# A graph network kernel: gathers without a clear in front, for the first window groups of two layers

## What is computed

```python
edge_index = jnp.stack([src, dst])
x = _layernorm(x + _L0_gnn_ref(x, edge_weight, edge_attr_3, ...), axis=-1)     # radial messages, summed by dst
x = _layernorm(x + _L1_gnn_ref(x, edge_index), axis=-1)                        # three hops of norm * x[src], summed by dst

# third layer: an MLP on (x[src], x[dst], edge_attr), maximum by dst
e_feat = jnp.concatenate([x[rol], x[col], edge_attr], axis=-1)
v = jax.nn.relu(e_feat @ W1 + b1) @ W2 + b2
out = jnp.maximum(jax.ops.segment_max(v, col, num_segments=num_nodes), x)

# fourth layer: attention over edges
en = (feat @ W2s + b2s)[src];  ev = (feat @ W2d + b2d)[dst]
e = jnp.sum(leaky_relu(en + ev) * attn, axis=-1, keepdims=True)
alpha = softmax of e over the edges of one dst
msg = jax.nn.softmax(en * r_feat * alpha, axis=-1)
rst = (feat + sum over heads of segment_sum(msg, dst)) @ W1 + b1
```

## Time and profile before

| | |
|---|---|
| median of 3 runs | 1805.34 us (1805.03 to 1808.98) |
| the profiled execution | 1798.87 us |
| its span | 1797.1 us |
| DVE busy | 1315.1 us, 73% |
| POOL busy | 1293.3 us, 72% |
| PE busy | 728.0 us, 41% |
| ACT busy | 483.4 us, 27% |
| clears (line 764) | 846 |
| gathers of layer A (work <- table) | 96, mean 1335 ns |
| gathers of layer B (A_msg <- table) | 96, mean 1198 ns |

### The profile page before, as it was taken

The page is one execution under the profiler, slowest core; times in us unless marked ns, Lnnn a source line. Parts: engine busy times, 40 slices in busy tenths (PEclk is TensorE's granted clock), DMA queues, the critical chain, the costliest instruction groups (busy, mean ns, idle before and its releaser), DMA issues.

```text
span 1797.1 us, 14406 instructions
## 1 busy us (share of the span) xinstructions
PE 728.0 (41%) x3676; PEld 543.9 (30%) x3676; DVE 1315.1 (73%) x2383; ACT 483.4 (27%) x1063; POOL 1293.3 (72%) x1871
## 2 busy tenths in 40 slices
PE   7920445455514006515434003266314776651500
PEld 3310212122202005415433003165313766651400
DVE  9952789899989978785657886388763989986300
ACT  7922311111101023514324212133201234432100
POOL 8877588788888858858888288860088847888776
PEclk9965778788757558859767555578656577765655
DMA  8156511111100123304223510000001111110000
GB/s 325 46 171 237 202 29 25 29 30 32 29 18 14 54 80 97 118 27 129 90 74 121 189 59 4 6 25 21 31 12 23 29 30 34 33 30 9 10 11 10
DMA packets 62302, 114.24 MB, mean 64 GB/s; under 512 B 25827, under 2 KB 46856, under 8 KB 61432
## 3 DMA queue, kind: packets, MB, share of 16 engines
q1 hardware_dynamic: 24432, 80.96, 12.4%
q0 software_dynamic: 31808, 12.77, 5.0%
q10 hardware_dynamic: 5960, 19.43, 3.0%
HBM read 61.13 MB, written 55.21 MB: 65 GB/s over the span
## 4 chain that ended last, share of the span: by engine, by line
POOL 54%; issue 17%; DVE 16%; PE 8%; ACT 2%; DMA 2%; another core or an unknown queue 0%; ACTq 0%; POOLq 0%; SPq 0%; DVEq 0%; PEld 0%; PEldq 0%
POOL out L917 12%; POOL joined L774 10%; POOL gtmp L764 7%; POOL A_dst L774 7%; POOL edge_sums L865 5%; POOL work L774 5%; PE bank L1296 4%; POOL A_msg L774 4%; POOL A_msg L859 3%; DVE work L1519 2%; DVE A_dst L1519 2%; DVE stat L1530 1%; DVE work L2306 1%; DVE joined L1519 1%; POOL out_short L774 1%
## 5 line engine op out<-in xcount | busy, mean ns | idle before, releaser
L764 POOL MEMSET gtmp<- 64x64 f32 x846 | 142.2, 168 | 199.7 <-DMA table<-A_dst 131.3
L1345 PE MATMUL bank<-w2fold,work 128*128 128x384 f32 x392 | 182.0, 607 | 200.0 <-DVE work L1519 183.1
L917 POOL DMA_INDIRECT out<-A_dst,out_i x196 | 217.4, 1109 | 59.5 <-POOL gtmp L764 33.8
L774 POOL DMA_INDIRECT A_dst<-in_x,dst_i x196 | 214.9, 1097 | 58.2 <-issue 29.9
L1530 DVE TENSOR_REDUCE work<-work 128x80 f32<-128x1280 f32 (+3 forms) x147 | 204.6, 1421 | 64.7 <-issue 36.7
L774 POOL DMA_INDIRECT joined<-x_pos,A_tmp x168 | 175.2, 1043 | 49.1 <-POOL gtmp L764 30.7
L1345 PEld LDWEIGHTS bank<-w2fold,work 128*128 128x128 f32 x392 | 85.8, 236 | 295.5 <-issue 250.3
L1519 DVE TENSOR_TENSOR work<-bank,work 128x384 f32<-128x384 f32 (+1 forms) x294 | 153.6, 589 | 0.2
L1012 ACT ACTIVATE work<-A_tmp,b1col,w1col 65x256 f32<-65x256 f32 x98 | 58.8, 600 | 341.5 <-PE bank L1345 275.2
L1383 PE MATMUL bank<-nodes_w,small 128*128 128x128 f32 (+1 forms) x784 | 118.6, 309 | 71.6 <-ACT small L1041 65.0
L774 POOL DMA_INDIRECT work<-table,pos_i x96 | 128.1, 1335 | 26.8 <-POOL gtmp L764 21.9
(11 more groups left out here) (394 smaller groups left out, 2162.9 us busy)
## 6 DMA issues: line engine op xcount, KB each, us to landing
work<-in_x SPq DMA_DIRECT2D x26, 960.0 KB
x_pos<-joined SPq DMA_DIRECT2D x13, 990.0 KB
out<-work ACTq DMA_DIRECT2D x13, 960.0 KB
A_tmp<-ew_turned_rows ACTq DMA_DIRECT2D x49, 130.0 KB
table<-A_dst SPq DMA_DIRECT2D x2, 3136.0 KB
edge_sums<-A_dst SPq DMA_DIRECT2D x2, 3136.0 KB
table<-A_dst SPq DMA_DIRECT2D x13, 448.0 KB
A_tmp<-in_edge_attr_2x SPq DMA_DIRECT2D x49, 112.0 KB
```

The lines of the kernel that those rows point to most:

```text
L764: pool.memset(tile, 0.0).then_inc(cleared, 1)
L774: pool.indirect_dma_start(out=column(t), out_offset=None, in_=of, in_offset=bass.IndirectOffsetOnAxis(ap=idx[:, t:t + 1], axis=0), bounds_ ...
L917: pool.indirect_dma_start(out=out, out_offset=bass.IndirectOffsetOnAxis(ap=out_i[:, t:t + 1], axis=0), in_=A_dst[:, t, :], in_offset=None, ...
L1345: last = nc.tensor.matmul(banks[2 * (u % PAIRS_DEEP) + j][:, 0:PATHS], hid_rows[:, u % PAIRS_DEEP, j * P:(j + 1) * P], w2_rows[:], start=T ...
```

## The change

A tuple of two counts is added, and the edited call passes no tile to clear for the first 2 windows of layer A (32 gathers) and the first window of layer B (16 gathers). The other 144 gathers of both layers keep their clears, as does everything else.

```diff
 SHIFT_BITS = 6
+UNCLEARED = (2, 1)
...
                     if i >= SLOTS:
                         pool.wait_ge(here, window_count(k - 3, i - SLOTS))
                     gather(lambda t: of[:, t, :], tables[k], pos_i, edge_limit, lambda t: here,
-                           range(first, first + slots), cleared_tile=gtmp[0:HF])
+                           range(first, first + slots), cleared_tile=None if i < UNCLEARED[k - 3] else gtmp[0:HF])
```

## The result

The changed kernel takes 1798.73 us (median of 9 runs, 1793.88 to 1803.57), the kernel before 1808.98 us beside it (9 runs, 1805.03 to 1811.7). The ratio is 0.9949 with a 95% interval of 0.9934 to 0.9965: 9.2 us faster, between 6.3 and 11.9 (the two medians alone differ by 10.3).

What follows compares the result with a forecast made beforehand. GpSimd's row of indirect transfers was taken as the bound, with VectorE waiting for gathers in both stretches; 5.8 us in A plus 2.6 in B, 8.4 off 1805.3, gave 1796.9 us, eight-in-ten range 1793.5 to 1802.2.

Steps and rivals of the forecast that it cites:

- The price of a clear: Beside a quiet VectorE 0.14 us (1.44 against 1.30 a step); beside the scans 0.23 us, uncleared step 1.38.
- The prediction's sign of being wrong: In the edited stretches: gathers without a clear taking over 1.35 us beside the scans would refute the forecast.
- Stretch A: Layer A's 32 uncleared gathers: four more get through before the long VectorE instruction at 1084.12, gaining 5.8 us.
- the alternative, three gathers: Layer A: if 0.5 us of small holds come between 1065 and 1084, the gain is only 4.3 us.
- the first gate: Layer A's 6.69 us VectorE instruction, holding a gather until 0.87 to 0.89 us past its end; eighth gather caught, before the seventh.
- Stretch B: Layer B's 16 uncleared gathers: the 17th starts at 1328.5 against 1331.13, gaining 2.6 us, bounds 1.8 to 3.4.
- The waits: VectorE's second waits for gathers in A and B end 5.8 and 8.4 us earlier and shorten by these amounts.
- The shift to the end: After each layer's second wait for gathers, both savings reach the kernel's end in full, as pure shifts.
- Sum: Whole kernel: 5.8 us in A plus 2.6 in B give 8.4 us, so 1805.3 becomes 1796.9 us.
- Rival 1: Long VectorE instructions in A and B catch the same gathers as before; gain only 3.2 us, 1802.1 us; chance 0.14.
- Rivals 2 and 3: Uncleared gathers step at 1.66 us, 1815.9 us (chance 0.05); close gathers lock VectorE out in A, some 1812 (0.03).
- The chance of 0.08 for slower: Whole kernel: probability given to a slowdown, from gathers falling into step with VectorE or locking it out.

Runs made afterwards that it cites:

- b_only: Against the kernel before, only the 16 clears of layer B's first window are gone; ratio 0.9979 (0.9965 to 0.9992).
- all_ab: Against the kernel before, no clear in front of any of the 192 gathers of layers A and B; ratio 1.0239 (1.0221 to 1.0257).
- no_clears: Against the kernel before, all 846 clears and their waits gone; ratio 1.2232 (1.2209 to 1.2255).
- ab_52: Against the kernel before, no clears for all five groups of layer A and the first two of layer B; ratio 0.9924 (0.9909 to 0.9938).

## Why the prediction was right

**The price of a clear** stands: 1.30 us between uncleared gathers beside a quiet DVE, and 1.37 beside the 32 scans (1056.31 to 1057.68) where 1.38 was said. The mechanism given for the latter was wrong in detail: gathers are not held to a multiple of 0.46, each takes 1.07 us instead of 1.00. The prediction's sign of being wrong, over 1.35 us beside the scans, can only have meant the gather itself, since its step was forecast at 1.38.

**Stretch A** came out at the alternative, three gathers (4.3 us) and not four (5.8). Measured from the first long instruction, it is 4.6 us. Two terms failed, both ahead of the first gate, and the second follows from the first. The first gather was put 0.5 us earlier without its clear; it starts 4.52 us after the 6.69 us reduction does (1032.28 to 1036.80), and before it was 4.56 (1028.58 to 1033.14): the clear in front of a gather that has to wait for its table anyway is free. And the next six gathers took 10.97 us where 10.2 was said, with two holds of 2.63 and 2.29 us: half a microsecond later than forecast, the third gather (1039.46) no longer gets through before DVE's 128x1696 instructions begin (1039.30), and is held instead of the fourth. So the seventh gather was caught (1047.77, 6.78 us), as before, not the eighth. From there the count was right: 25 gathers go through, and the second gate falls on the 33rd, which has its clear again (1088.47, 6.60 us), where it fell on the 30th. Both long gates let go 0.87 to 0.89 us after DVE's instruction ends, as the prediction read them: 1054.55 against 1053.68, and 1095.07 against 1094.19.

**Stretch B**: 2.6 us forecast, 2.6 measured. POOL's lines for it in after:

```profile
1299.86 4.52 POOL L775 DMA_INDIRECT A_msg<-table,pos_i  x1 [97.82 <-issue]
...
1323.68 1.00 POOL L775 DMA_INDIRECT A_msg<-table,pos_i  x1 [0.30 <-issue]
1324.67 0.17 POOL L765 MEMSET gtmp<- 64x64 f32 x1
1325.11 1.00 POOL L775 DMA_INDIRECT A_msg<-table,pos_i  x1 [0.27 <-POOL gtmp L765]
1326.12 0.17 POOL L765 MEMSET gtmp<- 64x64 f32 x1
1327.63 1.00 POOL L775 DMA_INDIRECT A_msg<-table,pos_i  x1 [1.35 <-issue]
```

The 17th gather starts at 1325.11; set against each layer's long instruction (1296.81 and 1300.11) it is 2.7 us earlier than the one at 1331.13.

**The waits** did not shorten as said (26.8 to some 21). In A the first one did, from 15.45 to 9.55 us, and the second is longer, 28.27 us: DVE comes to it 6.0 us earlier and leaves it 4.6 us earlier. In B both are shorter, 15.10 and 15.56 us against 17.96 and 17.30.

**The shift to the end** holds: after the second wait of A, 138.3 us pass to B's long instruction in after and 140.6 in before. That further 2.3 us is not the change's: b_only, which leaves A as it was, has 138.4. From B's second wait to the end of the span it is 403.3 us in before and 404.2 in after.

**Sum.** 8.4 us forecast; 7.2 read from the stretches, 9.2 (6.3 to 11.9) timed. That the timed gain comes out above the forecast, and the stretches below, means that the close match of the number is in part luck: A's term was 1.2 us too large. The forecast for the median, 1796.9 us, is 1.8 under the measured 1798.73. The kernel before took 1808.98 in this comparison, not the 1805.34 from which the 8.4 was taken off; from there it would have been 1800.6, 1.9 over.

**The rivals.** Rival 1 (3.2 us) saw one thing correctly, that the first gate would catch the same gather; it was wrong that the second would. Rivals 2 and 3 did not occur: no uncleared gather outside a gate goes in step with DVE at 1.66, and the 32 scans keep their place. The chance of 0.08 for slower was however argued from the wrong mechanisms. What makes more of the same edit cost time is the standstill of the others, and the sign of it was there in the trace of before, in DVE's timeline beside a later row of gathers without clears:

```profile
165.94 0.09 DVE L1775 MEMSET nodes_t<- 32x32 f32 x1 [2.53 <-remote]
168.72 0.09 DVE L1775 MEMSET nodes_t<- 32x32 f32 x1 [2.69 <-issue]
170.12 0.09 DVE L1775 MEMSET nodes_t<- 32x32 f32 x1 [1.32 <-issue]
171.52 0.09 DVE L1775 MEMSET nodes_t<- 32x32 f32 x1 [1.32 <-issue]
```

Instructions of 0.09 us, 1.4 or 2.8 us apart, with POOL's gathers 1.30 us apart beside them. I read these as short idle times of an engine that is not the bound. Longer ones in B (77.8 us in the three before PE's results) are more than the loss of all_ab there (52.8 us). That 48 clears can go without this is something the prediction had no reason for. In B one can be read from the traces: the 16 uncleared gathers are over at 1324.67 (the end of the last one), and PE's first matmuls of the quads come at 1336.59. The next 16 already meet them. In A the 32 are over at 1088.04, before the quads too, but that is not what saves A, since in all_ab PE and ACT work through the quads beside uncleared gathers.

## What to carry to other kernels

A redundant instruction between indirect transfers on GpSimd may be what lets the other engines go on: before taking such ones out, look in the trace at what the others do beside a row of transfers that has none, take them out stretch by stretch, and keep those out that bring no idle time without a named cause on the other engines; here that is layer A and the first group of B, 0.9924. A gap shorter than the engine's own issue time is worth only the difference (0.14 of 0.44 us), and where another engine's instruction holds the row, it counts in whole gathers. Measure a small saving inside its own stretch, from the last common instruction: with identical work ahead, the stretches' starts lay 18 us apart.

## What the runs showed of the hardware

Gathers on GpSimd of 128 indices, each 1.30 us after the one before, bring PE, ACT and DVE to a little over a third of their work in the first layer (no_clears, 250 to 400 us); with a clear on GpSimd between them, 0.14 us more a step, DVE does 196 instructions there against 72, and the same gathers with a semaphore increment and wait in between and no added time are no better (1.2296 against 1.2232). In the two-hop layer gathers at the same 1.30 us do not slow them (138 matmuls in 30 us), and a standstill that has begun goes on beside gathers with clears (ab_52, up to 1381.86). The DVE instruction with two inputs in SBUF that holds a gather until 0.87 us past its end works that way also with uncleared gathers.

PE and ACT, too, stand still in it: up to 2.59 us of idle time before each of several 0.21 us matmuls in all_ab. The Trainium skill ("SBUF — State Buffer", Who interferes with whom) says that only the pair of ports shared by VectorE and GpSimd contends and that "PE and ACT never wait on anyone". As a rule on ports this may stand; as a rule on time the measurement decides against it here: they wait, for a cause that no run names.
